# Graph attention layer in split single precision: the keys of heads 2 and 3 made and rounded inside the product with the weights, and the row sums of the last head half a tile later

## What is computed

```python
c_adj = mean(x, channels)
A = abs(abs(sigmoid(c_adj[m] - c_adj[n]) - 0.5) - 0.5) * 2.0
Wg = adj * (A + A.T) * 0.5                      # 1024 x 1024, the "weights"
g = relu((x.T @ Wg) * para)                     # 256 x 1024, gives q of four heads
k, v = split(x @ kv_w)                          # 1024 x 64 per head each
attn = softmax(q @ k.T * scale)                 # per head, 1024 x 1024
out = attn @ v
x1 = layernorm(x + out)
```

## Time and profile before

| what | value |
|---|---|
| median of three runs | 2922.38 us (2921.91 to 2923.61) |
| the profiled execution, its own time | 2922.4 us |
| its span, first to last instruction | 2920.6 us |
| mean granted clock of TensorE | 0.976 of full speed |
| TensorE busy, matmuls | 2734.2 us, 94% of the span |
| VectorE busy | 1979.5 us, 68% |
| ScalarE busy | 1658.2 us, 57% |
| GpSimd busy | 1280.7 us, 44% |
| one batch of the attention layer | 124.57 us (between the row sums at 904.87 and those at 1029.44) |

### The profile page before, as it was taken

The page is one execution under the profiler, slowest core; times in us unless marked ns, Lnnn a source line. Parts: engine busy times, 40 slices in busy tenths (PEclk is TensorE's granted clock), DMA queues, the critical chain, the costliest instruction groups (busy, mean ns, idle before and its releaser), DMA issues. The chain is left out here.

```text
span 2920.6 us, 39408 instructions
## 1 busy us (share of the span) xinstructions
PE 2734.2 (94%) x12436; PEld 1848.1 (63%) x12436; DVE 1979.5 (68%) x2821; ACT 1658.2 (57%) x2148; POOL 1280.7 (44%) x700
## 2 busy tenths in 40 slices
PE   7999999999999999999999999996799999989953
PEld 5565665656656566565656656563688888868843
DVE  6787786877868778686877868773533433248877
ACT  6666576666667666576665757653422222237757
POOL 3755657565475755757566475645200000000034
PEclk9999999999999999999999999998899999999976
DMA  4123222232222232222232222221322232215547
GB/s 137 58 87 98 76 72 79 65 104 86 69 71 79 82 99 75 76 72 79 77 99 83 72 70 74 86 70 53 110 87 86 100 107 94 86 43 187 173 179 282
DMA packets 125646, 276.20 MB, mean 95 GB/s; under 512 B 12192, under 2 KB 62368, under 8 KB 119456
## 3 DMA queue, kind: packets, MB, share of 16 engines
q1 hardware_dynamic: 125600, 275.62, 29.6%
HBM read 178.79 MB, written 62.98 MB: 83 GB/s over the span
## 5 line engine op out<-in xcount | busy, mean ns | idle before, releaser
L304 POOL TENSOR_TENSOR psum<-psum,probs 128x1024 f32<-128x1024 f32 x320 | 784.1, 2450 | 149.4 <-ACT probs L372 130.1
L372 ACT ACTIVATE probs<-sc_ps 128x1024 f32<-128x1024 f32 x512 | 505.6, 1023 | 419.5 <-PE sc_ps L815 358.3
L544 DVE TENSOR_REDUCE mx<-mx_ps 128x1 f32<-128x512 f32 x768 | 521.5, 690 | 318.1 <-PE mx_ps L784 316.5
L831 PE MATMUL pv_ps<-probs,v 128*64 128x512 f32 x2048 | 492.4, 604 | 0.0
L815 PE MATMUL sc_ps<-qa,ka 128*128 128x512 f32 x1024 | 386.8, 403 | 0.0
L815 PE MATMUL sc_ps<-qb,kb 128*128 128x512 f32 x1024 | 380.9, 395 | 0.5
L784 PE MATMUL mx_ps<-ka,qa 128*128 128x512 f32 x768 | 316.5, 422 | 8.6 <-DVE mx L544 3.1
L831 PEld LDWEIGHTS pv_ps<-probs,v 128*64 128x64 f32 x2048 | 125.6, 136 | 224.6 <-issue 194.3
L815 PEld LDWEIGHTS sc_ps<-qa,ka 128*128 128x128 f32 x1024 | 187.5, 188 | 105.6 <-issue 64.1
L1170 DVE TENSOR_TENSOR agg_lo<-ag_ps,agg_hi 128x1024 fp32r<-128x1024 f32 x32 | 39.2, 1225 | 313.5 <-ACT agg_hi L1097 313.4
L784 PEld LDWEIGHTS mx_ps<-ka,qa 128*128 128x128 f32 x768 | 139.8, 187 | 173.3 <-issue 77.9
(11 more groups left out here) (180 smaller groups left out, 5552.8 us busy)
## 6 DMA issues: line engine op xcount, KB each, us to landing
adj_ring<-in_adj_dram SPq DMA_DIRECT2D x128, 512.0 KB, 3.7
pre_scratch<-pre SPq DMA_DIRECT2D x28, 1024.0 KB, 4.5
pre<-pre_scratch SPq DMA_DIRECT2D x28, 1024.0 KB, 4.9
x<-in_x_dram SPq DMA_DIRECT2D x16, 1024.0 KB, 5.6
kb<-ka SPq DMA_DIRECT2D x64, 256.0 KB, 3.4
qa<-qa SPq DMA_DIRECT2D x64, 256.0 KB, 3.1
res<-in_x_dram SPq DMA_DIRECT2D x16, 1024.0 KB, 5.6
x_scratch<-res SPq DMA_DIRECT2D x16, 1024.0 KB, 4.5
```

The lines of the kernel that those rows point to most:

```text
L304: pool.tensor_tensor(psum[:, h % 2, :], probs[:, 0, :] if k == 1 else psum[:, h % 2, :], probs[:, k % PR, :], ALU.add).then_inc(s["pool_ad ...
L372: nc.scalar.activation(probs[:, i % PR, :], sc_ps[:, t % 2, :], ACT.Exp, scale=SCALE)\
L544: nc.vector.tensor_reduce(mx2[:, nh, n:n + 1], mx_ps[:, nh, :], AX.X, ALU.max)\
L831: ins = nc.tensor.matmul(pv_ps[nh * HD:(nh + 1) * HD, h % 2, :], v[:, i, h * HD:(h + 1) * HD], probs[:, i % PR, nh * BANK:(nh + 1) * BANK] ...
```

## The change

It has these parts:

- The keys of heads 2 and 3 are no longer four pieces into `pv_ps` behind the product, but one `k_product(b, 1)` of 12 matmuls into `mx_ps`, behind tile n = 1 of the product stage.
- ScalarE's `k_high(b, 2)`, `k_high(b, 3)` stand between `w_high(b, 6)` and `w_high(b, 7)`; VectorE's `k_low(b, 2)`, `k_low(b, 3)` between `w_low(b, 6)` and `w_low(b, 7)`. VectorE's `weigh(b, 7)` stands ahead of `add_head`.
- `sum_up` of the last head stands behind both channel halves of tile n = 1.
- In the stage of the maxima one tile of v_product(b, 0) stands ahead of the first rough scores, and all four tiles of v_product(b, 1) ahead of `transpose_maxima`.
- The first row of `MAX_HALVES` puts two rough-score matmuls of head 1 ahead of the first part 1 of `scores`, for head 0.
- On ScalarE `v_copy(b, 0)` stands ahead of `relu_q(b, 1)`, and six instead of four tiles of `x_high` ahead of `v_copy(b, 1)`.

```diff
-    MAX_HALVES = [[[0, 1, 1], [2, 1, 1, 1, 1], [2, 1, 1, 1, 1], [1, 1, 0, 0, 0]]] + \
+    MAX_HALVES = [[[2, 1, 1], [1, 1, 1, 1, 0], [2, 1, 1, 1, 1], [1, 1, 0, 0, 0]]] + \
...
                 w_high(b, 6)
+                k_high(b, 2)
+                k_high(b, 3)
                 w_high(b, 7)
                 q_high(b, 0)
                 q_high(b, 1)
                 relu_q(b, 0)
                 q_high(b, 2)
                 q_high(b, 3)
-                k_high(b, 2)
-                k_high(b, 3)
+                v_copy(b, 0)
                 relu_q(b, 1)
                 if not last:
-                    x_high(b + 1, range(0, 4))
-                v_copy(b, 0)
+                    x_high(b + 1, range(0, 6))
+                v_copy(b, 1)
                 if not last:
-                    x_high(b + 1, range(4, T))
-                v_copy(b, 1)
+                    x_high(b + 1, range(6, T))
...
                 weigh(b, 6)
                 w_low(b, 5)
+                weigh(b, 7)
                 if before:
                     add_head(b - 1, HEADS - 1)
-                weigh(b, 7)
                 w_low(b, 6)
+                k_low(b, 2)
+                k_low(b, 3)
                 w_low(b, 7)
...
-                maxima(b, 0, range(0, 4))
-                k_low(b, 2)
-                maxima(b, 0, range(4, 5))
-                k_low(b, 3)
-                maxima(b, 0, range(5, T))
+                maxima(b, 0, range(T))
...
-                        if before and n == 1 and c == 0:
-                            sum_up(b - 1, HEADS - 1)
                     ins.then_inc(s["g_step"], 1)
+                    if before and n == 1:
+                        sum_up(b - 1, HEADS - 1)
+                    if n == 1:
+                        k_product(b, 1)
...
             def body(b, last):
                 g_product(b)
-                k_piece(b, 0, 0)
-                k_piece(b, 0, 1)
+                v_product(b, 0, [0])
                 max_scores(b, 0, 0)
                 max_scores(b, 0, 1)
-                k_piece(b, 1, 0)
-                max_scores(b, 0, 2)
-                k_piece(b, 1, 1)
-                max_scores(b, 0, 3)
-                for m in range(4):
+                for m in range(1, 4):
                     v_product(b, 0, [m])
-                    max_scores(b, 0, 4 + m)
-                v_product(b, 1, [0, 1])
+                    max_scores(b, 0, m + 1)
+                max_scores(b, 0, 5)
+                v_product(b, 1, [0])
+                max_scores(b, 0, 6)
+                v_product(b, 1, [1])
+                max_scores(b, 0, 7)
+                v_product(b, 1, [2, 3])
                 transpose_maxima(b, 0)
-
-                v_product(b, 1, [2, 3])
                 scores(b, 0, 0, [0])
                 scores(b, 0, 1, [0])
```

More of the change, by code:

```diff
@@ L342, in k_high @@
                 wait(act, s["k_ready"], 2 * b + h // 2 + 1)
-                src = (mx_ps, pv_ps)[h // 2]
-                nc.scalar.activation(ka[h][own(h), :], src[own(h), :, :].rearrange("p a n -> p (a n)"), ACT.Copy)\
+                nc.scalar.activation(ka[h][own(h), :], mx_ps[own(h), :, :].rearrange("p a n -> p (a n)"), ACT.Copy)\
                     .then_inc(s["kh_done"], 1)
@@ L521, in k_low @@
                 wait(dve, s["kh_done"], 4 * b + h + 1)
-                src = (mx_ps, pv_ps)[h // 2]
-                nc.vector.tensor_tensor(ka[h][other(h), :], src[own(h), :, :].rearrange("p a n -> p (a n)"),
+                nc.vector.tensor_tensor(ka[h][other(h), :], mx_ps[own(h), :, :].rearrange("p a n -> p (a n)"),
                                         ka[h][own(h), :].bitcast(F32), ALU.subtract).then_inc(s["kl_done"], 1)
@@ L705, in k_terms, with k_product @@
                                     for k in range(CT)])
-            def k_product(b):
-                wait(pe, s["xtl_done"], 2 * b + 2)
-                wait(pe, s["row_done"], 4 * b)
+            def k_product(b, c):
+                if c == 0:
+                    wait(pe, s["xtl_done"], 2 * b + 2)
+                    wait(pe, s["row_done"], 4 * b)
+                else:
+                    wait(pe, s["kl_done"], 4 * b + 2)
                 for nh in range(NH):
-                    ins = product(mx_ps[:, nh, :], k_terms(0, nh))
+                    ins = product(mx_ps[:, nh, :], k_terms(c, nh))
                 ins.then_inc(s["k_ready"], 1)
[L714 to L722, removed]
             def v_product(b, j, tiles=range(4)):
                 if j == 0:
-                    wait(pe, s["kl_done"], 4 * b + 2)
+                    wait(pe, s["kl_done"], 4 * b + 4)
                 else:
@@ L824, in values @@
                 wait(pe, s["exp_done"], 32 * b + t + 1)
-                if i == 0 and h < 2:
+                if i == 0:
                     wait(pe, s["v_evac"], 2 * b + 2)
-                    wait(pe, s["kl_done"], 4 * b + 4)
-                elif i == 0:
                     wait(pe, s["res_added"], 4 * b + h - 1)
@@ L867, in prepare @@
                 if (h, p) == (3, 2):
-                    k_product(b)
+                    k_product(b, 0)
             def body(b, last):
                 g_product(b)
-                k_piece(b, 0, 0)
-                k_piece(b, 0, 1)
+                v_product(b, 0, [0])
                 max_scores(b, 0, 0)
                 max_scores(b, 0, 1)
-                k_piece(b, 1, 0)
-                max_scores(b, 0, 2)
-                k_piece(b, 1, 1)
-                max_scores(b, 0, 3)
-                for m in range(4):
-                    v_product(b, 0, [m])
-                    max_scores(b, 0, 4 + m)
-                v_product(b, 1, [0, 1])
+                for m in range(1, 4):
+                    v_product(b, 0, [m])
+                    max_scores(b, 0, m + 1)
[5 more added lines that the diff above has]
+                v_product(b, 1, [2, 3])
                 transpose_maxima(b, 0)
-                v_product(b, 1, [2, 3])
                 scores(b, 0, 0, [0])
@@ L930, in _ @@
             pe.wait_ge(s["consts_set"], 3)
-            k_product(0)
+            k_product(0, 0)
             pe.wait_ge(s["kq_set"], 2 * HEADS)
```

## The result

| | before | changed |
|---|---|---|
| median | 2922.48 us (2921.91 to 2923.61, 4 runs) | 3017.65 us (3009.50 to 3022.96, 4 runs) |
| span of the profiled execution | 2920.6 us | 3007.7 us |
| mean granted clock | 0.976 | 0.940 |

The changed kernel is slower: ratio 1.0323, 95% interval 1.0299 to 1.0346. The spans differ by 87.1 us. The profiled execution of the changed kernel is the fastest of its four; the others took 8 to 14 us more, at a mean clock of 0.935 to 0.937. The page of the changed kernel shows the first sign, where the earlier trace rows stood for before: TensorE's share is the same 94%, but with 80 us more busy time for the same matmuls, and the granted clock has eights all through the loop.

What follows compares the result with a forecast made beforehand. TensorE's order, busy 94% of the span, was taken as the bound. Terms of 2.9 - 1.95 - 1.0 = -0.05 us in 15 batches and -4.2 in the first gave -5 us: 2917.5 us, range 2910 to 2925 (0.56).

Steps and rivals of the forecast that it cites:

- The wait for the row sums: Product stage: six matmuls ahead of the last head's sums remove TensorE's 1.06 us wait, gaining 1.14 us in 15 batches.
- First rough scores: Head 0, behind the product: they start 2.9 us later because VectorE reaches `q_times_para` late.
- From there to the transpose: First rough scores to the transpose of the maxima: 11.1 us instead of 13.05, 1.95 us shorter.
- To part 1: Transpose of the maxima to part 1 of the scores: kept at 2.65 us, TensorE idle for about 1 us.
- To the values: Part 1 of the scores to the first values of head 0: 4.65 us, where it was 5.64.
- VectorE is in time: Rival: `q_times_para` starts with its operand, 1.55 us earlier a batch, 23 us more gained, 2894 us; chance 0.14.
- the tile by tile hand-over: Rival: round trips between rough scores and maxima set the pace, stage shrinks 1 us, +14 us, 2931 us; chance 0.18.
- the row sums did not hold TensorE: Rival it denies: in the product, VectorE's late addition still makes TensorE wait, +16 us, 2933 us; chance 0.05.
- The first batch: Batch without one before it: 2.95 us from later stretches plus 1.3 us of saved clock loss, -4.2 us.
- the keys are free: First batch: the moved keys fill TensorE's 5.29 us wait for tile 3's weights, leaving 2.5 us idle.
- `mx_ps` free, long done: Product stage: the twelve moved key matmuls, 2.75 us, need only transposed x and this free buffer, so add no wait.
- The clock falls: Rival: 2 us idle ahead of the rough scores lowers TensorE's clock each batch, 1.7 us each, +25 us, 2943 us; chance 0.07.

Runs made afterwards that it cites:

- the run with the gap in the product: The kernel before with four more BN_STATS on VectorE ahead of the addition for head 3's row sums, inside the product: 2952.67 us, ratio 1.0109.
- the other form of `neg_mean`: The changed kernel with statistics and moments split and moved later on VectorE, two small TENSOR_SCALAR rewritten as TENSOR_TENSOR and SCALAR_TENSOR_TENSOR: 2957.17 us, ratio 1.0117.
- row sums alone: The kernel before with only the move of the last head's row sums behind both halves of tile 1: 2918.55 us, again 2916.55 us.

## Why the prediction was wrong

**The terms of the loop were right, but for the clock.** The wait for the row sums went, and these start 1.68 us behind the common row (forecast 1.68). First rough scores: forecast +2.9, measured +3.10. From there to the transpose: 11.1, measured 11.09. To part 1: 2.65 and 2.65. To the values: 4.65, measured 4.76. Together -0.05 forecast, +0.26 measured. VectorE without idle time ahead of `q_times_para` and TensorE idle "some 2 us" (2.10) came as predicted. One dependency I missed: part 0 of the scores waits for the negated row (0.67 us); it cost nothing, since part 1 sets the pace. Neither "VectorE is in time" nor the tile by tile hand-over happened, and the row sums did not hold TensorE.

**The first batch was wrong, by 3.3 us.** I counted -4.2, with "the keys are free" in the 5.29 us wait for weights; its first rough scores should have come 1.3 us earlier and came 2.0 later (55.50 against 53.54). In the changed kernel the keys themselves wait, for the low parts of the first two heads' keys in the same PSUM tile, and the clock is low behind this wait too (0.50 over the next 4.08 us, by the windows). "`mx_ps` free, long done" holds in the loop only:

```profile
32.92 0.80 PE L677 MATMUL mx_ps<-xT_hi,kvw_hi 128*128 128x512 f32 x1 [5.07 <-DVE ka L521]
```

The first rough scores of batch 1 come at 180.24, 2.21 us later than the 178.03 of before; with +3.10 for the stretch ahead of them the first batch had gained 0.9.

**The step that failed is the granted clock in the loop.** The sum has no term for it: it was left at nothing there and stood only in the rival "The clock falls". That was the right mechanism, with the wrong chance (0.07) and the wrong price (1.7 us a batch). The price came from the windows of the earlier trace rows, where 512-column products follow a fall; the run with the gap in the product shows that there it is indeed 1.3 to 1.6 us. I carried it to a place with other work behind it, where it was 7.1 to 9.6 us, and the clock fell in ten of fifteen batches. The chance had only two rows under it, 5.29 us with a fall and 1.06 without, and my 2 us "between": that is a coin toss by the rows, not one case in fourteen. With this price and a coin toss for the chance, the slower side alone would have held half. The ten falls cost 85 us (77.7 + 7.2) of the 87.1 us between the spans. All the rest of the sum was off by 8 us: 0.31 us a batch in the loop and the 3.3 us of the first batch.

The rule of the Trainium skill that I had set beside this rival (TensorE: Matmul & The Clock Gate, the part on the clock gate: an idle spell brings back the half rate) points to the side that came. The trace agrees in ten of the fifteen cases behind 2.10 us of idle time; in the other five the clock stayed at 1.00. But I had read it short: the same part warns of idle gaps longer than this one. Read whole, it did not say that the change would be the slower one. Where the two differ the measurement decides.

## What to carry to other kernels

An idle stretch on TensorE has two prices, its length and the clock behind it, and the second can be three to six times the first (7.1 to 9.6 us behind 2.1, 7.1 to 8.2 behind 1.4); before moving work off TensorE ahead of a stretch of small matmuls, see whether the stretch leaves it idle, and price a fall from the stage that follows, not from another. Where an engine is late anyway, useless matmuls in the gap are a quick test for this (82 us here), and an ordering that has no gap is the cure. Operations of VectorE on SBUF, small or big, can be held for as long as a running sum of GpSimd lasts when they start behind it; the statistics were not, so look at the rows of each before placing it.

## What the runs showed of the hardware

- The lower clock, once granted, stayed while TensorE worked on rough scores and values: it covered most of 18.5 us (0.52 to 0.57) at 17.81 to 18.50 us of busy time. In the product, and at the end of the stage behind the last rough scores, it was over within 6 us (0.72).
- An idle stretch of 1.4 us was followed by a fall in 11 of 15 cases, of 1.8 us in 7, of 2.1 us in 10, of 2.4 us inside the product in 5, of 2.6 us inside head 0 in 10 of 14 and, with the other form of `neg_mean`, 8 of 14, of 4.2 us there in 15 of 15. Behind 0.8 us at the last rough scores it fell in 2 and in 1 of 16 (row sums alone), behind 0.7 us at the first ones in none. At one length of idle time the clock both fell and stayed, so what else decides in a single case is open; it was not only the length.
- VectorE's `neg_mean` on 128x8 took 2.31 us in place of 0.17, and its addition of 128x1024 3.35 us in place of 1.22, when a running sum of GpSimd (2.35 us) had started 0.08 to 0.09 us ahead.
